# Depthwise convolution of an attention block moved from GpSimd to TensorE, as diagonal matmuls into the bank of the weighted terms

## The chip, the cores and the metric

One core of one Trainium2 chip runs the whole kernel. The metric is the device time of one execution in microseconds (us), taken as the median of several runs. The engines are named as the profile names them: PE is TensorE (PEld its weight loads), DVE is VectorE, ACT is ScalarE, POOL is GpSimd, SP is the engine that issues the DMAs (SPq is its queue). L1195 is line 1195 of the kernel before.

## The reference

The input `x` is (4, 1024, 128): four sequences, which the kernel calls batches, of 1024 tokens and 128 channels in 8 heads of 16. All is float32.

```python
def _ripple(x, Wqkv, Wo, conv_w):
    q, k, v = jnp.split(x @ Wqkv, 3, axis=-1)
    # tele: each token attends to the tokens 0, 1, 2, 4, ... 512 back
    sc = jnp.einsum('bhsd,bhskd->bhsk', qh, kg) / np.sqrt(d)
    w = jax.nn.softmax(jnp.where(valid, sc, -jnp.inf), axis=-1)
    tele = jnp.einsum('bhsk,bhskd->bhsd', w, vg)
    # conv: causal depthwise convolution of v with 7 taps per channel
    vpad = jnp.pad(v, ((0, 0), (KCONV - 1, 0), (0, 0)))
    conv = conv_general_dilated(vpad, conv_w, feature_group_count=c)
    # low: linear attention
    fq, fk = elu(qh) + 1.0, elu(kh) + 1.0
    kv = einsum('bhsd,bhse->bhde', fk, vh)
    low = einsum('bhsd,bhde->bhse', fq, kv) / (z[..., None] + 1e-06)
    return (tele + conv_h + low) @ Wo
x = x + layernorm(xn + _ripple(xn, ...))     # xn = layernorm(x)
x = x + layernorm(moe(layernorm(x)))         # 8 experts of 64, top 2, and a shared one
```

The change is about `conv` alone: `conv[t, c]` is the sum over seven taps of `conv_w[c, tap] * v[t - 6 + tap, c]`.

## The kernel before, in words

Every engine has a program of its own, written out by hand; semaphores join them. The loop runs over five steps `b`. Step `b` holds the attention of batch `b` (steps 0 to 3) and the expert network of batch `b - 1` (steps 1 to 4), cut in two units of 512 tokens, `u0 = 2b - 2` and `u1 = 2b - 1`. The projections of the next batch are made within the step as well. I call the step by its batch.

The attention of a batch has two parts, and the text uses these names for them.

- **The front**, up to the low terms. DVE and POOL multiply q with shifted k (`products`, L263), PE sums them over heads (`sum_heads`, L1163), turns the scores (L1105), DVE makes the softmax (`softmax_logits`, `softmax_weights`, L836 to L856). In the same stretch DVE works through the 24 small steps of the gates of unit u0 (`gates`, L935 to L985, 128x32 elements each), after which PE turns the gates (`gates_expert_major`, L1266), spreads them (`spread_gates`, L1278) and DVE multiplies (`gate_hidden`, L994). `low` (L1181) puts the linear attention into the banks psH and psY, and `weigh_low` (L864) takes it out again and signals `low_used`.
- **The term stage**, from `low_used` on. PE first writes the experts' output of u0 (`experts_out`, L1292, 20 matmuls into psY). Then, tile by tile for eight tiles of 128 tokens, DVE multiplies v with the weights (`weigh`, L880; four sets of buffers, so it can be four tiles ahead) and PE turns and adds the 9 to 12 terms of the tile in psH (`sum_terms`, L1192 and L1195). psH holds four tiles, so it is filled twice, in a first and a second half. After each half `add_conv` (L897, DVE) adds psH and the convolution and writes hT, and `output` (L1206) multiplies it with Wo. Between the tiles PE also runs `project_q`, `project_v` of the next batch, and `hidden`, `gates_expert_major` and `spread_gates` of u1.

`weigh` reads `v_shift`: copies of the token-major v (`v_tok`), shifted by 1 to 64 tokens, which 14 DMAs on SP's queue make (`shift_v`, L339 and L340) as soon as ACT has written `v_tok` at the very end of the batch before. Its first tile waits for all of them.

The convolution runs on POOL, in transposed layout (channels on the partitions): `conv_start` multiplies vT with the last tap, `conv_taps` makes a product (L457, 128x1024) and an addition (L460) for each of the six others, thirteen operations in a chain (`conv_step`). It stands behind `ln3(u1)` in POOL's order. DVE's `add_conv` and ACT's `evacuate_v` of the next batch, which overwrites vT, wait for it.

PSUM is full: psA, psG and psF have two banks each, psH and psY one.

Of the kernel before, what the change touches and what calls it, by code (L numbers as in the profile page):

```python
# [16 lines left out]
ALU = mybir.AluOpType  # L17
# [46 lines left out]
N_CONV_STEPS = 2 * TAPS - 1  # L64
# [49 lines left out]
def block_kernel(nc, x, Wqkv, Wo, conv_w, gate_W, W1, b1, W2, b2, Ws1, bs1, Ws2, bs2, route_scale, out):  # L114
# [4 lines left out]
    with ExitStack() as ctx:  # L119
# [71 lines left out]
        convT = sb("convT", [P, T])  # L191
        tapT = sb("tapT", [P, T])
# [50 lines left out]
        conv_step, hT_ready, y_ready, yc_ready = sem("conv_step"), sem("hT_ready"), sem("y_ready"), sem("yc_ready")  # L243
# [10 lines left out]
        conv_chain = Chain(conv_step, N_CONV_STEPS)  # L254
# [112 lines left out]
        def _(pool):  # L367
# [30 lines left out]
            def more_constants():  # L398
# [18 lines left out]
                nc.gpsimd.memset(neg_half[0:1, 0:1], -0.5).then_inc(consts_ready, 1)  # L417
# [26 lines left out]

            def conv_start(b):
                pool.wait_ge(psA_free, freed(b - 1, PSA_V, 1))
                if b == 0:
                    pool.wait_ge(conv_ld, 16)
                else:
                    pool.wait_ge(hT_ready, upto(b, 2, 0))  # L450
                conv_chain.start(pool, b)
                conv_chain(nc.gpsimd.tensor_scalar(convT[:], vT[:, VPRE:VPRE + T], cw[:, TAPS - 1:TAPS], 0.0,
                                                   ALU.mult, ALU.add))

            def conv_taps(b, shifts):
                for shift in shifts:
                    conv_chain(nc.gpsimd.tensor_scalar(tapT[:], vT[:, VPRE - shift:VPRE - shift + T],  # L457
                                                       cw[:, TAPS - 1 - shift:TAPS - shift], 0.0,
                                                       ALU.mult, ALU.add))
                    conv_chain(nc.gpsimd.tensor_tensor(convT[:], convT[:], tapT[:], ALU.add))  # L460
# [33 lines left out]
            for b in range(B + 1):  # L494
# [12 lines left out]
                if attn:  # L507
                    conv_start(b)
                    conv_taps(b, range(1, TAPS))
                    conv_chain.done()  # L510
# [17 lines left out]
        def _(act):  # L528
# [34 lines left out]
            def evacuate_v(b):  # L563
                act.wait_ge(conv_step, upto(b, N_CONV_STEPS, 0))
                for half in range(2):
                    evacuate(b - 1, PSA_V, half, vT[:, VPRE + half * HALF:VPRE + (half + 1) * HALF])

            def features(b):
# [5 lines left out]
                nc.scalar.activation(fqT[:], qT[:], ACT.Relu).then_inc(q_feat, 1)  # L574

# [104 lines left out]
            for b in range(B + 1):  # L680
# [3 lines left out]
                if attn:  # L684
# [38 lines left out]
                    if ffn:  # L723
                        hidden(u1, range(2, 4))
                        shared_hidden(u1)
# [706 lines left out]
```

## Time and profile before

| | |
|---|---|
| time, median of 3 runs | 341.28 us (341.16 to 342.54) |
| profiled execution: its span, the only time it gives | 339.5 us |
| PE busy | 261.4 us, 77% |
| DVE busy | 275.6 us, 81% |
| ACT busy | 176.8 us, 52% |
| POOL busy | 196.6 us, 58% |
| POOL in L460, the convolution's additions | 57.9 us, 24 of 2412 ns |
| POOL in L457, its products | 30.1 us, 24 of 1255 ns |
| mean granted TensorE clock | 0.874 of full |

A busy share is the part of the span in which the engine had an instruction in work; an instruction that is held by something inside the engine counts as busy, so a small operation with a long duration is a held one. "[2.60 <-DVE gparts L985]" behind a row says that the engine had stood idle for 2.60 us and that DVE's line 985, which writes gparts, ended it. The time outside the profiled span is the difference of the first two lines, 1.8 us; it is taken to stay.

### The profile page before, as it was taken

Reading aid. Unit: us, or ns where it says so; the run is one execution under the profiler, and the core shown is the slowest. Engines: PE = TensorE matmul, PEld = TensorE weight load, DVE = VectorE, ACT = ScalarE, POOL = GpSimd, SP = SyncE. Lnnn points to the kernel's source line nnn. Section 1 sums busy time; section 2 is a strip of 40 time slices with the busy share of each in tenths; the row PEclk is TensorE's granted clock in tenths of the full one; section 3 lists DMA queues with packets and bytes.
Section 4 is the critical chain, followed back from the end, with each engine's and each line's share of the span. In section 5 each row is a group of like instructions: output and inputs, shape, how many; then the busy total and the mean of one; then the engine's idle time right before and its main releaser. Section 6 shows DMA issues by size and latency. Waiting matters only on the chain.

```text
span 339.5 us, 4554 instructions
## 1 busy us (share of the span) xinstructions
PE 261.4 (77%) x1527; PEld 175.7 (52%) x1527; DVE 275.6 (81%) x555; ACT 176.8 (52%) x443; POOL 196.6 (58%) x193
## 2 busy tenths in 40 slices
PE   6666667089379699997788499998795878888894
PEld 6323342087334537667455237767443277685374
DVE  5079866188999999989999999989999999845752
ACT  1683055302538755593569344775484606176852
POOL 4960999601889995306899980327979943131013
PEclk9785996569879959999999659999999559989999
DMA  7200376000025700200049300100248200000003
GB/s 219 71 0 16 106 196 147 24 0 3 9 90 143 215 26 8 69 26 3 37 130 229 111 12 2 31 2 8 84 124 215 83 12 31 0 2 0 2 2 93
DMA packets 20038, 21.89 MB, mean 64 GB/s; under 512 B 3289, under 2 KB 16434, under 8 KB 20014
## 3 DMA queue, kind: packets, MB, share of 16 engines
q1 hardware_dynamic: 20014, 21.59, 22.9%
q8 instruction: 12, 0.20, 0.2%
q14 instruction: 12, 0.10, 0.1%
HBM read 5.07 MB, written 2.10 MB: 21 GB/s over the span
## 4 chain that ended last, share of the span: by engine, by line
DVE 48%; PE 24%; ACT 9%; SPq 7%; DMA 6%; issue 4%; POOL 2%; POOLq 0%; DVEq 0%; ACTq 0%
DVE prods L263 12%; PE psH L1195 7%; DVE prods L880 6%; SPq L340 5%; DMA v_shift<-v_tok 5%; PE psA L1113 3%; DVE hid L994 3%; PE psY L1206 2%; PE psY L1292 2%; PE psA L1105 2%; DVE wgt L853 2%; PE psG L1278 2%; DVE gtmp L966 2%; SPq L339 2%; DVE gtmp L979 2%
## 5 line engine op out<-in xcount | busy, mean ns | idle before, releaser
L421 POOL TENSOR_SCALAR var<-ss 128x4 f32<-128x4 f32 (+1 forms) x25 | 13.4, 538 | 98.9 <-ACT squares L603 46.6
L263 DVE TENSOR_TENSOR prods<-qT,kT 128x1024 f32<-128x1024 f32 x32 | 55.4, 1778 | 12.4 <-ACT qT L530 12.4
L460 POOL TENSOR_TENSOR convT<-convT,tapT 128x1024 f32<-128x1024 f32 x24 | 57.9, 2412 | 2.0
L1195 PE MATMUL psH<-ident,prods 128*128 128x128 f32 x324 | 44.6, 290 | 0.0
L263 POOL TENSOR_TENSOR prods<-qT,kT 128x1024 f32<-128x1024 f32 (+1 forms) x12 | 28.8, 2418 | 23.2 <-PE psA L1163 11.3
L1195 PEld LDWEIGHTS psH<-ident,prods 128*128 128x128 f32 x324 | 40.5, 152 | 2.3 <-issue 2.3
L423 POOL TENSOR_TENSOR rstd<-var,neg_half 128x4 f32<-128x4 f32 (+2 forms) x29 | 37.8, 1305 | 2.4
L1163 PE MATMUL psA<-prods,slot_sel 128*32 128x512 f32 x168 | 26.0, 676 | 12.9 <-DVE prods L263 12.6
L880 DVE TENSOR_TENSOR prods<-v_shift,wgt 128x896 f32<-128x896 f32 x32 | 34.7, 1083 | 0.0
L880 DVE TENSOR_TENSOR prods<-v_tok,wgt 128x128 f32<-128x128 f32 (+2 forms) x60 | 25.8, 456 | 9.9 <-DMA v_shift<-v_tok 9.9
L1113 PE MATMUL psA<-xnT,wqkv 128*128 128x512 f32 x48 | 29.9, 767 | 5.0 <-ACT xnT L530 5.0
L457 POOL TENSOR_SCALAR tapT<-vT,cw 128x1024 f32<-128x1024 f32 x24 | 30.1, 1255 | 2.4
L1256 PE MATMUL psF<-x3T,w 128*128 128x512 f32 x58 | 31.2, 650 | 0.1
L994 DVE TENSOR_TENSOR hid<-hid,psG 128x512 f32<-128x512 f32 x32 | 20.7, 681 | 9.7 <-PE psG L1278 9.1
L1192 PE MATMUL psH<-ident,prods 128*128 128x128 f32 x32 | 9.9, 308 | 15.4 <-DVE prods L880 11.9
L1292 PEld LDWEIGHTS psY<-w,hid 128*128 128x128 f32 x140 | 18.2, 215 | 6.4 <-DVE prods L864 6.4
L1292 PE MATMUL psY<-w,hid 128*128 128x128 f32 x140 | 18.9, 300 | 3.3 <-DVE prods L864 3.3
L603 ACT ACTIVATE squares<-yc 128x128 f32<-128x128 f32 x32 | 9.4, 297 | 22.4 <-DVE yc L903 22.4
L638 ACT ACTIVATE hid<-psF,b1c 128x512 f32<-128x512 f32 x29 | 18.8, 684 | 2.5 <-PE psF L1256 2.4
L1113 PEld LDWEIGHTS psA<-xnT,wqkv 128*128 128x128 f32 x48 | 10.5, 242 | 17.3 <-ACT xnT L530 7.5
L1256 PEld LDWEIGHTS psF<-x3T,w 128*128 128x128 f32 x58 | 10.7, 206 | 13.9 <-issue 13.0
L1163 PEld LDWEIGHTS psA<-prods,slot_sel 128*32 128x32 f32 x168 | 5.3, 118 | 23.5 <-DVE prods L263 13.5
(194 smaller groups left out, 581.3 us busy)
## 6 DMA issues: line engine op xcount, KB each, us to landing
x_in<-L_attn_x SPq DMA_DIRECT2D x4, 512.0 KB, 4.0
x_res<-L_attn_x SPq DMA_DIRECT2D x4, 512.0 KB, 15.3
v_shift<-v_tok SPq DMA_DIRECT2D x4, 508.0 KB
v_shift<-v_tok SPq DMA_DIRECT2D x4, 504.0 KB
v_shift<-v_tok SPq DMA_DIRECT2D x4, 496.0 KB
v_shift<-v_tok SPq DMA_DIRECT2D x4, 480.0 KB
v_shift<-v_tok SPq DMA_DIRECT2D x4, 448.0 KB
out<-y_out SPq DMA_DIRECT2D x7, 256.0 KB, 2.3
```

The source lines that it names most:

```text
L263: return eng.tensor_tensor(prods[:, QUADS * (s % 2) + q, t0:T], qT[:, t0:T], kT[:, PRE - off + t0:PRE - off + T], ALU.mult)
L423: return nc.gpsimd.tensor_tensor(rstd[:, cols], var[:, cols], neg_half[:, cols], ALU.pow)
L457: conv_chain(nc.gpsimd.tensor_scalar(tapT[:], vT[:, VPRE - shift:VPRE - shift + T], cw[:, TAPS - 1 - shift:TAPS - shift], 0.0, ALU.mult, A ...
L460: conv_chain(nc.gpsimd.tensor_tensor(convT[:], convT[:], tapT[:], ALU.add))
L638: nc.scalar.activation(hid[:, c, half_cols(u)], hidden_bank(u, c), ACT.Gelu, bias=b1c[:, c:c + 1]).then_inc(hidden_free, 1)
L880: return nc.vector.tensor_tensor(dst, src.rearrange("p m (h d) -> p m h d", d=HD), w, ALU.mult)
L994: nc.vector.tensor_tensor(hid[:, c, cols], hid[:, c, cols], psG[:, c % 2, :], ALU.mult).then_inc(gated, 1)
L1113: pe.matmul(psA[:, half, :], wqkv[:, bass.ts(part, P)], xnT[:, bass.ts(half, HALF)], start=True, stop=True).then_inc(psA_full, 1)
L1163: ins = pe.matmul(psA[32 * q:32 * q + 32, half, :], ksum_sel[:] if low else slot_sel[:, s, :], fqT[:, cols] if low else prods[:, QUADS * ( ...
L1195: ins = pe.matmul(dst, terms[:, j % TERM_BUFS, m, :], ident[:], is_transpose=True, start=False, stop=(m == live[-1]))
L1256: pe.matmul(hidden_bank(u, c), w1[:, bass.ts(c, P)], x3T[:, half_cols(u)], start=True, stop=True).then_inc(hidden_full, 1)
L1292: ins = pe.matmul(output_tile(u, n), hid[:, c, bass.ts(j, P)], w2[:, c, :], start=(c == CH - 1), stop=(c == CH - 2))
```

## The change

Seven diagonal matrices `tap_diag[:, tap, :]`, the identity times one tap's weights, are made once on POOL. For each half, `sum_conv` has PE multiply them with vT, shifted by the tap, over 512 columns of psH, the first of the seven with `start=True`; the terms of the four tiles are then added on top (`start=False`). `evacuate_h` on ACT copies the sum from psH to hT; `add_conv` is gone from DVE, and the thirteen operations on POOL are gone for each batch. `evacuate_v` waits for `conv_summed` instead.

```diff
@@ POOL, more_constants
-                nc.gpsimd.memset(neg_half[0:1, 0:1], -0.5).then_inc(consts_ready, 1)
+                pool.wait_ge(conv_ld, 16)
+                pool.wait_ge(ident_ready, 1)
+                for tap in range(TAPS):
+                    ins = nc.gpsimd.tensor_scalar(tap_diag[:, tap, :], ident[:], cw[:, tap:tap + 1], 0.0, ALU.mult, ALU.add)
+                ins.then_inc(consts_ready, 1)
...
-                if attn:
-                    conv_start(b)
-                    conv_taps(b, range(1, TAPS))
-                    conv_chain.done()
@@ ACT
+            def evacuate_h(b, half):
+                act.wait_ge(terms_summed, upto(b, NT, TPH * (half + 1)))
+                copy(hT[:, bass.ts(half, HALF)], psH[:]).then_inc(hT_ready, 1)
...
                         shared_hidden(u1)
+                    evacuate_h(b, 0)
+                    if ffn:
                         gates_expert_major(u1)
                         gate_rows(u1)
                     if more:
                         features(b + 1)
                     norm2(2 * b)
+                    evacuate_h(b, 1)
                     if not more:
                         norm3_squares(2 * b)
@@ DVE
-                        if j == TPH:
-                            add_conv(b, 0)
...
                     residual(2 * b)
-                    add_conv(b, 1)
@@ PE
+            def sum_conv(b, half):
+                if half:
+                    pe.wait_ge(hT_ready, upto(b, 2, 1))
+                else:
+                    pe.wait_ge(low_used, b + 1)
+                    if b == 0:
+                        pe.wait_ge(consts_ready, 2)
+                for tap in range(TAPS):
+                    t0 = VPRE - (TAPS - 1 - tap) + half * HALF
+                    ins = pe.matmul(psH[:], tap_diag[:, tap, :], vT[:, t0:t0 + HALF], start=(tap == 0), stop=False)
+                if half:
+                    ins.then_inc(conv_summed, 1)
...
+                        if j % TPH == 0:
+                            sum_conv(b, j // TPH)
                         sum_terms(b, j)
```

On PE, in the term stage of batch 1, the order before is this, from the experts' output to the output of the first half (L1292 are the experts, L1192 and L1195 a tile's terms, L1266 the turned gates, L1206 the output):

```order
L1292 MATMUL psY<-w,hid 128x128 x20
L1192 MATMUL psH<-ident,prods 128x128
L1195 MATMUL psH<-ident,prods 128x128 x8
L1113 MATMUL psA<-xnT,wqkv 128x512 x2
...
L1266 MATMUL psG<-identb,gparts 24x128 x4
L1192 MATMUL psH<-ident,prods 128x128
L1195 MATMUL psH<-ident,prods 128x128 x11
L1206 MATMUL psY<-wo,prods 128x128 x4
```

After the change the same place reads as follows (its lines are those of the changed kernel: L1280 the experts, L1172 the convolution, L1180 and L1183 the terms):

```order
L1280 MATMUL psY<-w,hid 128x128 x20
L1172 MATMUL psH<-vT,tap_diag 128x512 x7
L1180 MATMUL psH<-ident,prods 128x128
L1183 MATMUL psH<-ident,prods 128x128 x8
L1091 MATMUL psA<-xnT,wqkv 128x512 x2
...
L1254 MATMUL psG<-identb,gparts 24x128 x4
L1172 MATMUL psH<-vT,tap_diag 128x512 x7
L1180 MATMUL psH<-ident,prods 128x128
L1183 MATMUL psH<-ident,prods 128x128 x11
L1194 MATMUL psY<-wo,prods 128x128 x4
```

Seven matmuls of 512 columns stand in front of each half's first tile, behind the experts' output in the one place and behind the turned gates in the other.

On ACT, at the end of the term stage, the order before is this (L530 is the copy helper; L603 are the squares of the second norm, L570 to L574 the features of the next batch):

```order
L642 ACTIVATE hid<-gate_shared,bs1c 64x512
L530 ACTIVATE gT<-psG 24x512
L530 ACTIVATE hid<-gT 24x512
L570 ACT_TABLE_LOAD
L570 ACTIVATE kexp<-kT 128x1024
L571 ACTIVATE fkT<-kT 128x1024
L572 ACTIVATE qexp<-qT 128x1024
L574 ACTIVATE fqT<-qT 128x1024
L603 ACTIVATE squares,ss<-yc 128x128 x4
L530 ACTIVATE vT<-psA 128x512 x2
L530 ACTIVATE v_tok<-psA 128x512 x2
```

And after the change:

```order
L626 ACTIVATE hid<-gate_shared,bs1c 64x512
L510 ACTIVATE prods<-psH 128x512
L510 ACTIVATE gT<-psG 24x512
L510 ACTIVATE hid<-gT 24x512
L550 ACT_TABLE_LOAD
L550 ACTIVATE kexp<-kT 128x1024
L551 ACTIVATE fkT<-kT 128x1024
L552 ACTIVATE qexp<-qT 128x1024
L554 ACTIVATE fqT<-qT 128x1024
L587 ACTIVATE squares,ss<-yc 128x128 x4
L510 ACTIVATE prods<-psH 128x512
L510 ACTIVATE vT<-psA 128x512 x2
```

Two copies from psH have come in (hT lies in the space of prods and is named so): one in front of the gates' copy, one in front of the copy of vT.

## Rows read from the trace of the kernel before

**Rows 1.** Page: the span; the engines' shares of the last chain.

```profile
span 339.5 us, 4554 instructions
DVE 48%; PE 24%; ACT 9%; SPq 7%; DMA 6%; issue 4%; POOL 2%; POOLq 0%; DVEq 0%; ACTq 0%
```

**Rows 2.** Windows of batch 1's front and term stage: engines' busy us.

```profile
88.00:130.20 42.20, 31.83 (x157) 15.83 (x154) 40.53 (x70) 26.84 (x66) 38.86 (x27) 0.80 0.34 98
130.20:158.70 28.50, 25.24 (x177) 19.82 (x177) 26.72 (x63) 16.81 (x39) 7.64 (x8) 1.00 0.10 29
```

**Rows 3.** Timeline of DVE and POOL in batch 2's front: start, us, instruction.

```profile
179.08 1.12 POOL L452 TENSOR_SCALAR convT<-vT,cw 128x1024 f32<-128x1024 f32 x1
179.18 1.06 DVE L949 TENSOR_TENSOR gtmp<-gtmp,gmax 128x32 f32<-128x32 f32 x1
...
189.19 2.21 DVE L983 TENSOR_TENSOR gtmp<-gtmp,gparts 128x32 f32<-128x32 f32 x1
```

**Rows 4.** Timeline of PE: the gate turn, batches 1 to 3.

```profile
117.51 0.39 PE L1266 MATMUL psG<-identb,gparts 128*24 128x128 bf16 x4 [2.60 <-DVE gparts L985]
...
191.77 0.58 PE L1266 MATMUL psG<-identb,gparts 128*24 128x128 bf16 x4 [6.19 <-DVE gparts L985]
...
261.07 0.38 PE L1266 MATMUL psG<-identb,gparts 128*24 128x128 bf16 x4 [3.02 <-DVE gparts L985]
```

**Rows 5.** Timeline of PE: the experts' output, batches 1 to 3.

```profile
130.34 4.73 PE L1292 MATMUL psY<-w,hid 128*128 128x128 f32 x40
...
205.73 4.73 PE L1292 MATMUL psY<-w,hid 128*128 128x128 f32 x40 [0.59 <-DVE prods L864]
...
273.80 7.04 PE L1292 MATMUL psY<-w,hid 128*128 128x128 f32 x40 [2.75 <-DVE prods L864]
```

**Rows 6.** Timeline of PE: 512-column matmuls at either clock.

```profile
125.13 3.64 PE L1113 MATMUL psA<-xnT,wqkv 128*128 128x512 f32 x4 [0.78 <-ACT xnT L530]
...
138.71 1.88 PE L1256 MATMUL psF<-x3T,w 128*128 128x512 f32 x4
140.42 0.27 PE L1192 MATMUL psH<-ident,prods 128*128 128x128 f32 x1
```

**Rows 7.** Window in batch 1; last columns: PEclk, DMA share, GB/s.

```profile
126.00:127.00 1.00, 1.00 (x3) 0.34 (x2) 0.93 (x3) 0.00 (x0) 1.00 (x1) 0.50 0.07 28
```

**Rows 8.** Timelines of PE, DVE and SP: the wait for v_shift.

```profile
67.84 0.47 PE L1192 MATMUL psH<-ident,prods 128*128 128x128 f32 x1 [9.85 <-DVE prods L880]
...
66.49 0.29 DVE L880 TENSOR_TENSOR prods<-v_tok,wgt 128x128 f32<-128x128 f32 x1 [9.91 <-DMA v_shift<-v_tok]
...
26.09 0.72 SPq L339 DMA_DIRECT2D v_shift<-v_tok  x1
...
87.97 0.71 SPq L339 DMA_DIRECT2D v_shift<-v_tok  x1
...
158.75 0.70 SPq L339 DMA_DIRECT2D v_shift<-v_tok  x1
```

**Rows 9.** Timelines of PE and DVE: the second half's sums.

```profile
142.40 0.33 PE L1192 MATMUL psH<-ident,prods 128*128 128x128 f32 x1 [0.61 <-DVE prods L880]
...
145.07 0.30 PE L1192 MATMUL psH<-ident,prods 128*128 128x128 f32 x1 [0.93 <-DVE prods L897]
...
219.25 0.30 PE L1192 MATMUL psH<-ident,prods 128*128 128x128 f32 x1 [0.55 <-DVE prods L897]
...
155.21 0.68 DVE L897 TENSOR_TENSOR prods<-psH,convT 128x512 f32<-128x512 f32 x1
```

**Rows 10.** Timeline of ACT: a copy of half a bank; batch 3's end.

```profile
136.96 0.60 ACT L530 ACTIVATE qT<-psA 128x512 f32<-128x512 f32 x1 [0.70 <-PE psA L1113]
...
299.64 1.28 ACT L734 ACT_TABLE_LOAD   x1
...
302.07 0.31 ACT L603 ACTIVATE squares<-yc 128x128 f32<-128x128 f32 x1 [0.94 <-DVE yc L903]
```

**Rows 11.** Timeline of POOL: batch 0's first products.

```profile
19.08 4.57 POOL L263 TENSOR_TENSOR prods<-qT,kT 128x512 f32<-128x512 f32 x2 [1.38 <-ACT qT L530]
```

More of the change, by code:

```diff
@@ L63 @@
 N_SOFTMAX_STEPS = 5
-N_CONV_STEPS = 2 * TAPS - 1
 N_FRONT = 3
@@ L190, in block_kernel @@
         prods = sb("prods", [P, 2 * QUADS, T])
-        convT = sb("convT", [P, T])
-        tapT = sb("tapT", [P, T])
+        tap_diag = sb("tap_diag", [P, TAPS, P])
         space = prods[:].rearrange("p a t -> p (a t)")
@@ L242, in block_kernel @@
         terms_ready, terms_summed = sem("terms_ready"), sem("terms_summed")
-        conv_step, hT_ready, y_ready, yc_ready = sem("conv_step"), sem("hT_ready"), sem("y_ready"), sem("yc_ready")
+        conv_summed, hT_ready, y_ready, yc_ready = sem("conv_summed"), sem("hT_ready"), sem("y_ready"), sem("yc_ready")
         ss2_ready, x2_ready, ss3_ready, xn3_ready = sem("ss2_ready"), sem("x2_ready"), sem("ss3_ready"), sem("xn3_ready")
@@ L253, in block_kernel @@
         softmax_chain = Chain(softmax_step, N_SOFTMAX_STEPS)
-        conv_chain = Chain(conv_step, N_CONV_STEPS)
         def bank(tile):
@@ L443, in products @@
                             product(nc.gpsimd, s, q).then_inc(pool_prod_ready, 1)
[L445 to L460, printed above, removed]
             def ln2(u):
@@ L563, in evacuate_v @@
             def evacuate_v(b):
-                act.wait_ge(conv_step, upto(b, N_CONV_STEPS, 0))
+                act.wait_ge(conv_summed, upto(b, 1, 0))
                 for half in range(2):
@@ L891, in weigh @@
                 beside(2)
-            def add_conv(b, half):
-                dve.wait_ge(terms_summed, upto(b, NT, TPH * (half + 1)))
-                dve.wait_ge(conv_step, upto(b, N_CONV_STEPS, N_CONV_STEPS))
-                cols = bass.ts(half, HALF)
-                nc.vector.tensor_tensor(hT[:, cols], psH[:], convT[:, cols], ALU.add).then_inc(hT_ready, 1)
             def add_normed(b, half):
@@ L1182, in low @@
                 ins.then_inc(low_ready, 1)
+            def sum_conv(b, half):
[10 more added lines that the diff above has]
+                    ins.then_inc(conv_summed, 1)
             def sum_terms(b, j):
                 pe.wait_ge(terms_ready, upto(b, NT, j + 1))
-                if j == 0:
-                    pe.wait_ge(low_used, b + 1)
-                elif j == TPH:
-                    pe.wait_ge(hT_ready, upto(b, 2, 1))
                 dst = psH[:, bass.ts(j % TPH, P)]
-                pe.matmul(dst, low_terms[:, j, :], ident[:], is_transpose=True, start=True, stop=False)
+                pe.matmul(dst, low_terms[:, j, :], ident[:], is_transpose=True, start=False, stop=False)
                 live = [m for m in range(NV) if TERMS[m] < P or TERMS[m] // P <= j]
@@ L1195, in sum_terms @@
                     ins = pe.matmul(dst, terms[:, j % TERM_BUFS, m, :], ident[:], is_transpose=True,
-                                    start=False, stop=(m == live[-1]))
+                                    start=False, stop=(m == live[-1] and j % TPH == TPH - 1))
                 ins.then_inc(terms_summed, 1)
```

## The prediction

> **What bounds the kernel now.** I read the page first: the span is 339.5 us, and in the chain that ended last DVE has 48% and PE 24% [rows 1], POOL hardly any. So POOL's 88 us of convolution are not on the chain by themselves. The windows then tell two kinds of stretch apart [rows 2]: in the front of batch 1 DVE is busy 40.5 of 42.2 us and PE 31.8 at a mean granted clock of 0.80; in the term stage that follows DVE is busy 26.7 and PE 25.2 of 28.5 at full clock. The reader is to see that PE has no room in the second stretch, which is where the change puts its matmuls, and that DVE seems to have none in the first.
>
> But part of DVE's time in the front is not work. In batch 2 a gate step of 128x32 elements takes 1.06 us and another 2.21; the first ends at 180.24, just when POOL's convolution operation, begun before it, ends (180.20) [rows 3]. A DVE operation with two SBUF inputs is held until POOL's ends. Seven of batch 2's steps are held, of which the rows show the first and the last. What this costs stands on PE: the turn of the gates came after 2.60, 6.19 and 3.02 us of idle time that the last gate step ended [rows 4]. Low terms are through when the experts' output starts: 130.34, 205.73 and 273.80 [rows 5].
>
> **The price of the new matmuls.** Four records of PE are two matmuls of 128x512, with different weights: they start at 138.71 and the next work at 140.42, so one matmul takes 0.86 us at full clock [rows 6]. Seven make 6.0 us a half, 12.0 a batch, 48 in all. At the low clock, granted clock 0.50, which is the 1.2 GHz level [rows 7], the same two took 3.64 [rows 6], so a half would cost up to 12.
>
> One page reads otherwise. The Trainium skill (TensorE: Matmul & The Clock Gate, Back-to-back issue gap) gives about 131 ns as the sustained spacing of matmuls of 512 columns; the row has 0.43 us for each record. By the page a half would cost 14 x 0.131 = 1.8 us and the sum would turn negative; by the row it is 6.0. The row is of this very shape and type, so the sum goes by it.
>
> **Batch 0.** The first half's convolution waits for low_used and the constants. PE is then idle for 9.85 us before 67.84, since the shifted copies land only at 66.49 [rows 8]; 6.0 us fit, cost nothing. Without that cover they would cost 6.0. The second half stands behind the first four tiles with only the wait for the copy before it, which stays: +6.0. PE's idle stretch is shorter, so the first tiles may run at the higher clock earlier; I take 0.5 off, bounds 0 and 2: **+5.5**.
>
> **Batch 1, front.** With POOL quiet, the last gate step is early and the 2.60 us in front of the gate turn go [rows 4]. They are all that goes: the turn cannot come before PE's work in front of it. From the turn (117.51) to low_used (130.2) it took 12.7. I rebuild this chain at full clock: turn and copy of the gates 1.2, two spreads 1.0, gate_logits 0.9, two spreads 1.0, last product 0.8, softmax sums and weights 4.0, low terms 1.3, together 10.2. These are estimates from the same operations at full clock; PE, with no idle time of 2.6 us there, should keep it, where before the clock was 0.50 [rows 7]. That gives 2.5 more, bounds 0 and 3. Low_used is 5.1 earlier. PE then does the experts' output and the first half's convolution, +6.0, so the first tile's sum starts 0.9 later than before. DVE has its terms ready by then: the copies took 40.4 us from the first issue to the use (26.09 to 66.49), so those issued from 87.97 land at 128.4 [rows 8], and with 2.4 for the first tile that is 5 us before the convolution's end at 136.0 (135.1 and 0.9).
>
> **Batch 1, term stage.** The second half costs 6.0 less what PE idled: 0.61 before the fourth tile and part of the 0.93 at the second half's first sum, where DVE's copy was late ([rows 9], against 0.55 in batch 2). I take 5.0, bounds 4.5 and 6. At the end add_conv stood behind the residual without idle time [rows 9]; ACT is free there, I take 0.5 off (bounds 0 and 1). Batch 1: 0.9 + 5.0 - 0.5 = **+5.4**.
>
> **Batch 2.** The turn gains 6.19 [rows 4], the chain behind it, 13.8 long, 3.5: low_used is 9.7 earlier, at 196. The copies, issued from 158.75 [rows 8], land at 199.2, before experts (4.7) and convolution (6.0) are through at 206.7. So -9.7 + 6.0 = -3.7; then +6.0 for the second half, whose wait of 0.55 [rows 9] stays, and -0.5: **+1.8**.
>
> **Batch 3.** The turn gains 3.02 [rows 4] and the chain 2.5: -5.5, and +6.0. The experts' output took 7.04 against 4.73 [rows 5], because PE had been idle 2.75 before; whether the clock holds this time is open, I take half of the 2.3: -1.2. Second half +6.0, less 1.3 for idle time and low clock at the last tiles (bounds 0 and 3): together **+4.0**.
>
> **The end.** ACT's copy of the last half takes 0.60 [rows 10] like DVE's addition, so the swap itself is nothing in the chain. But in batch 3 the squares and the table load (299.64, 1.28) now stand behind this copy instead of before the sum's end. Copy, four squares and table make about 3.9 us, where the squares of the last unit had started 2.8 after the last sum (302.07, with 0.94 idle, [rows 10]): **+1.1**, bounds 0 and 1.5.
>
> **Costed at nothing.** The seven diagonals on POOL: between nothing and 1.12 each (the 128x1024 form, [rows 3]), so at most 7.8 us after which POOL's first products, now at 19.08 [rows 11], come at most 6.5 late; batch 0's wait of 9.85 hides this, else it is that. ACT's copy of the first half waits in front of the gates' copy and, in batch 0, of the next batch's features; these are needed only at the batch's end. DVE loses eight operations of 0.68 [rows 9], off the path but for what is counted. Nobody waits for the time that POOL gets back.
>
> **Sum.** 5.5 + 5.4 + 1.8 + 4.0 + 1.1 = 17.8. The span becomes 357.3; with the 1.8 between the profiled span and the median, 359.1, that is 5% slower. In short: 48 us of PE work, of which 6 hide in batch 0, about 20 are paid by the front and about 4 by idle time and late copies.
>
> **The rivals.**
> - *The front gives nothing back*, because something else (ACT's work, or PE at the low clock) holds the chain to low_used at its old length. For it: PE's clock was 0.80 in the front [rows 2], and ACT has its own queue there. Against: three idle times are named after the gate step [rows 4]. Then the front's 5.1, 9.7 and 5.5 are lost too: 359.1 + 20.3 = 379. With the idle times alone gained, 11.8 of the 20.3, it is 367.6, which is still inside my case.
> - *The copies become the bound.* If they land later than 40.4 after issue by more than 5 us, each of three batches is later by the rest. One engine's share, 0.07, is all that moves at the end of a landing [rows 7]. The Trainium skill (DMA: Bandwidth & Descriptors, Why a DMA increments its semaphore by 16 and not by 1) says that a transfer over 127 partitions uses one engine; the trace agrees with the share of 0.07. I see nothing in the change that slows it; 3 us in each would give 368.
> - *The other side: a convolution matmul is cheaper than a projection's.* If 512 columns went at 0.13 us a record, a half costs 1.8 and the copies' landing bounds the fronts: first sums start 4.3, 8.9 and 4.3 earlier (landing plus 2.4 for the first tile, 130.8 and 201.6, against 135.1 and 210.5, [rows 5, 8]; batch 3 like batch 1), and the second halves cost 1.8 x 4 less about 1. With the end's 1.1, that is -17.5 + 6.2 + 1.1 = -10.2: 331. It decides from about 0.25 us a record on. For it speaks only the page cited above; against it every 512-column row.
> - *The held steps go on being held* by POOL's remaining work. Then it is the first rival.
>
> **How the numbers follow.** A difference under 0.5%, 1.7 us, is about what a measurement of this kernel can't tell from none. My case 0.84, front gives nothing 0.06, copies bound 0.05, the cheap matmul 0.04, anything else about even 0.01. Within my case the bounds add up as follows: all at their kind end (3.5 less in batch 0 and 3's clock, 3 in the last tiles and idle times, 1.1 at the end, 1.5 elsewhere) gives 350; the chain behind the turn not quickened (8.5 more), the low clock in batch 3 and no idle time regained (2.5) gives 370. The range 350 to 369 leaves out the far rivals and the edge. Slower 0.94, within 0.5% 0.02, faster 0.04.
>
> **What would show it.** PE busy up by about 45 us, to over 300; twice seven 512-column matmuls a batch at 0.86 us spacing; no gate step over 0.3 us while POOL is idle; low_used 5 to 10 us earlier relative to the batch's first copy issue; then no idle time on PE from the experts' output to the second half's end; the term stages longer by about 11 us in batches 1 to 3, by 6 in batch 0. Wrong would be the prediction if the fronts stay 42 to 47 us long (the chain isn't the gates'), if the new matmuls take 1.7 us (the clock falls), or if DVE and not PE ends the waits in the term stage.

## The result and the profile after

The changed kernel takes **359.87 us** (median of 4 runs, 358.91 to 360.02) where the kernel before took 341.62 in runs on the same chip: ratio 1.0542, interval 1.0502 to 1.0583. It is 5.4% slower. Its profiled span is 358.2 us, against 339.5 [rows 1].

The page of the changed kernel: the span, the engines' busy us with their shares and instructions, the chain that ended last, and the new matmuls as a group (busy us, mean ns, idle time before).

```profile
span 358.2 us, 4710 instructions
PE 298.7 (83%) x1639; PEld 190.2 (53%) x1639; DVE 237.2 (66%) x547; ACT 181.0 (51%) x451; POOL 112.3 (31%) x147
...
PE 53%; ACT 18%; DVE 11%; SPq 7%; DMA 6%; POOL 3%; issue 2%; POOLq 0%; DVEq 0%; ACTq 0%
...
L1172 PE MATMUL psH<-vT,tap_diag 128*128 128x512 f32 x112 | 49.8, 595 | 1.8 <-ACT prods L510 1.8
```

The chain has turned over: before, DVE had 48% and PE 24% [rows 1]; now PE has 53%. The new matmuls take 49.8 us and almost never wait; they are on the path, not in gaps.

The windows of the changed kernel: batch 1's stage from the experts to the next batch's first copy, and the last microseconds of the fronts of batches 1 and 2. After the busy times come PEclk, DMA share, GB/s.

```profile
131.10:169.50 38.40, 36.95 (x206) 25.02 (x204) 23.10 (x60) 17.82 (x41) 7.04 (x7) 1.00 0.08 23
126.00:130.00 4.00, 4.00 (x6) 1.70 (x7) 3.69 (x6) 1.44 (x3) 0.00 (x0) 0.57 0.06 26
202.00:208.00 6.00, 5.24 (x6) 2.19 (x7) 4.37 (x6) 3.18 (x6) 0.00 (x0) 0.50 0.34 109
```

The stage that took 28.5 us with both engines nearly full [rows 2] takes 38.4 us with PE at 96% and DVE at 60%. The two lower rows matter below: there the granted clock is at or near 0.50, the 1.2 GHz level.

The timeline of SyncE, the first copy of each batch, answers to the issues in [rows 8]; that of batch 3 stood at 233.08 before.

```profile
26.61 0.73 SPq L336 DMA_DIRECT2D v_shift<-v_tok  x1
...
92.96 0.70 SPq L336 DMA_DIRECT2D v_shift<-v_tok  x1
...
169.51 0.71 SPq L336 DMA_DIRECT2D v_shift<-v_tok  x1
...
247.30 0.71 SPq L336 DMA_DIRECT2D v_shift<-v_tok  x1
```

From issue to issue the batches grew by 4.5 (batch 0), 5.8 and 3.5 us; batch 3, to its last sum, by 4.0; the head and the end by 0.5 each. That is the 18.7 us of the span, with rounding.

The timeline of PE in the changed kernel, batch 1 (start, us, instruction, idle before and what ended it).

```profile
119.59 0.39 PE L1254 MATMUL psG<-identb,gparts 128*24 128x128 bf16 x4
...
122.16 1.10 PE L1223 MATMUL psF<-x3T,w 128*128 128x512 f32 x2 [0.62 <-ACT x3T L510]
...
124.71 0.41 PE L1228 MATMUL psF<-ident,gate_shared 8*128 8x8 f32 x4 [0.92 <-ACT gate_shared L510]
...
125.89 3.55 PE L1091 MATMUL psA<-xnT,wqkv 128*128 128x512 f32 x4 [0.77 <-ACT xnT L510]
129.24 2.05 PE L1244 MATMUL psF<-x3T,w 128*128 128x512 f32 x4
131.13 4.63 PE L1280 MATMUL psY<-w,hid 128*128 128x128 f32 x40
135.59 6.17 PE L1172 MATMUL psH<-vT,tap_diag 128*128 128x512 f32 x14
141.60 0.27 PE L1180 MATMUL psH<-ident,prods 128*128 128x128 f32 x1
...
150.37 6.28 PE L1172 MATMUL psH<-vT,tap_diag 128*128 128x512 f32 x14 [0.36 <-ACT prods L510]
```

Fourteen records are seven matmuls: 135.59 to 141.60 is 6.0 us a half, at full clock. The turn of the gates (L1254), which stood behind 2.60 us of idle time [rows 4], has none. In VectorE's timeline the low terms end here:

```profile
129.15 0.68 DVE L851 TENSOR_TENSOR prods<-psY,wgt 128x512 f32<-128x512 f32 x1
```

That is 129.83, 36.9 us behind the batch's first copy issue, where it was 42.3. But the experts start only at 131.13: PE was still at its own queue, projection and first hidden chunks at the low clock.

### The profile page after: what moved, and what is told of

Read it like the earlier page. It is cut to its first block, busy times and chain, and to the rows that moved or that the text cites. A ratio compares the mean times of both kernels' runs of the same rounds, so it can differ in the third digit from the quotient of the medians.

```text
span 358.2 us, 4710 instructions
## 1 busy us (share of the span) xinstructions
PE 298.7 (83%) x1639; PEld 190.2 (53%) x1639; DVE 237.2 (66%) x547; ACT 181.0 (51%) x451; POOL 112.3 (31%) x147
## 4 chain that ended last, share of the span: by engine, by line
PE 53%; ACT 18%; DVE 11%; SPq 7%; DMA 6%; POOL 3%; issue 2%; POOLq 0%; DVEq 0%; ACTq 0%
PE psH L1172 12%; PE psH L1183 10%; PE psA L1091 6%; DVE prods L260 5%; PE psY L1280 5%; SPq L337 5%; PE psF L1244 5%; DMA v_shift<-v_tok 5%; ACT xn L522 3%; PE psA L1141 2%; ACT xn L600 2%; PE psY L1194 2%; ACT prods L510 2%; SPq L336 2%; ACT hid L622 2%
## 5 line engine op out<-in xcount | busy, mean ns | idle before, releaser
L260 DVE TENSOR_TENSOR prods<-qT,kT 128x1024 f32<-128x1024 f32 x32 | 53.3, 1714 | 13.0 <-ACT qT L510 13.0
L1172 PE MATMUL psH<-vT,tap_diag 128*128 128x512 f32 x112 | 49.8, 595 | 1.8 <-ACT prods L510 1.8
L1183 PE MATMUL psH<-ident,prods 128*128 128x128 f32 x324 | 41.5, 278 | 0.0
L1183 PEld LDWEIGHTS psH<-ident,prods 128*128 128x128 f32 x324 | 37.7, 144 | 4.3 <-issue 4.3
L867 DVE TENSOR_TENSOR prods<-v_tok,wgt 128x128 f32<-128x128 f32 (+2 forms) x60 | 20.8, 373 | 26.6 <-DMA v_shift<-v_tok 23.0
L260 POOL TENSOR_TENSOR prods<-qT,kT 128x1024 f32<-128x1024 f32 (+1 forms) x12 | 30.9, 2591 | 19.6 <-PE psY L1194 11.7
L1172 PEld LDWEIGHTS psH<-vT,tap_diag 128*128 128x128 f32 x112 | 20.6, 189 | 26.1 <-issue 23.3
L1091 PE MATMUL psA<-xnT,wqkv 128*128 128x512 f32 x48 | 29.6, 762 | 3.3 <-ACT xnT L510 3.3
L510 ACT ACTIVATE prods<-psH 128x512 f32<-128x512 f32 x8 | 4.8, 597 | 35.4 <-PE psH L1183 35.4
L1280 PEld LDWEIGHTS psY<-w,hid 128*128 128x128 f32 x140 | 18.2, 212 | 3.4 <-DVE prods L851 2.4
L1280 PE MATMUL psY<-w,hid 128*128 128x128 f32 x140 | 18.5, 297 | 0.9 <-DVE prods L851 0.9
L1091 PEld LDWEIGHTS psA<-xnT,wqkv 128*128 128x128 f32 x48 | 10.1, 233 | 15.6 <-issue 6.3
## 6 DMA issues: line engine op xcount, KB each, us to landing
x_res<-L_attn_x SPq DMA_DIRECT2D x4, 512.0 KB, 15.5
```

The source lines that it names most:

```text
L260: return eng.tensor_tensor(prods[:, QUADS * (s % 2) + q, t0:T], qT[:, t0:T], kT[:, PRE - off + t0:PRE - off + T], ALU.mult)
L867: return nc.vector.tensor_tensor(dst, src.rearrange("p m (h d) -> p m h d", d=HD), w, ALU.mult)
L1091: pe.matmul(psA[:, half, :], wqkv[:, bass.ts(part, P)], xnT[:, bass.ts(half, HALF)], start=True, stop=True).then_inc(psA_full, 1)
L1172: ins = pe.matmul(psH[:], tap_diag[:, tap, :], vT[:, t0:t0 + HALF], start=(tap == 0), stop=False)
L1183: ins = pe.matmul(dst, terms[:, j % TERM_BUFS, m, :], ident[:], is_transpose=True, start=False, stop=(m == live[-1] and j % TPH == TPH - 1))
L1280: ins = pe.matmul(output_tile(u, n), hid[:, c, bass.ts(j, P)], w2[:, c, :], start=(c == CH - 1), stop=(c == CH - 2))
```

## The experiments

Each run's ratio is to the kernel before, run on the same chip; I turn differences of ratios into time with 340.3 us. "Relative" times are counted from the batch's first copy issue.

### 1. The old load back on GpSimd, the new matmuls kept

```diff
+        tapT = sb("tapT", [P, T])
...
+                if attn:
+                    conv_start(b)
+                    conv_taps(b, range(1, TAPS))
+                    conv_chain.done()
```

`conv_start` is one product and `conv_taps` six products and six additions, all within the one scratch buffer tapT, which nobody reads. The copy of the next batch's v waits for them again.

> The changed kernel, with POOL doing its old thirteen operations per batch again in their old place, into a scratch buffer that nobody reads (one buffer instead of two, for want of space; the result is that of the changed kernel). My theory: the fronts were shortened by 4.2, 7.6 and 5.8 us because POOL no longer holds DVE. All three come back, so the time is 359.9 + 17.6 = 377, between 372 and 380, with gate steps of 1 to 2.2 us and idle time on PE in front of the gate turn as before. Rival (the fronts are shorter because PE's clock or order changed, POOL has no part): 360, unchanged, with the gate steps held but the front as short.

Measured 371.0 us (370.05 to 372.38), ratio 1.0909 (1.086 to 1.0958): 12.5 us more than the change, some 5 short of the expectation. The timeline of PE in this kernel, the turn of the gates in batches 1 to 3:

```profile
122.77 0.39 PE L1275 MATMUL psG<-identb,gparts 128*24 128x128 bf16 x4 [1.68 <-DVE gparts L987]
...
205.65 0.58 PE L1275 MATMUL psG<-identb,gparts 128*24 128x128 bf16 x4 [4.83 <-DVE gparts L987]
...
283.85 0.38 PE L1275 MATMUL psG<-identb,gparts 128*24 128x128 bf16 x4 [2.09 <-DVE gparts L987]
```

The idle times of [rows 4] are back, a little smaller: 1.68, 4.83, 2.09 for 2.60, 6.19, 3.02. So is the hold of single steps; VectorE in batch 2:

```profile
197.22 1.55 DVE L964 TENSOR_TENSOR gtmp<-gtmp,gmax 128x32 f32<-128x32 f32 x1
198.81 0.19 DVE L966 TENSOR_TENSOR gtmp<-gtmp 128x32 f32<-128x32 f32 x1
```

A step of 128x32 takes 0.19 or, held, 0.78 to 1.77. That GpSimd's load lengthens the fronts, through held steps, is shown: with it the experts start 3.3, 5.0 and 3.5 us later behind the first copy issue than in the change, which had them 4.2, 7.6 and 5.8 us earlier than the kernel before. Why not all came back is argued and not shown: the 24 additions within one buffer took 1.98 us each, where the two-buffer ones had taken 2.41, so this load holds VectorE for less time than the real convolution did.

### 2. No convolution at all

```diff
-                for tap in range(TAPS):
-                    t0 = VPRE - (TAPS - 1 - tap) + half * HALF
-                    ins = pe.matmul(psH[:], tap_diag[:, tap, :], vT[:, t0:t0 + HALF], start=(tap == 0), stop=False)
                 if half:
+                    ins = pe.transpose(psH[:, 0:P], ident[:], ident[:])
...
```

The convolution's part of the output is missing here. Each tile's low terms start the bank themselves again, and one turn of the identity a batch stands for the signal.

> The changed kernel without the convolution: the 14 matmuls per batch are left out, the terms of each tile start the bank themselves; the output lacks conv. My theory: seven of the eight halves are on the path at 6.0 us each, 42 in all, of which the landing of the shifted copies, the first tiles' terms and DVE's pace take back 1 to 4: 320, between 316 and 325, which is 18 to 25 below the kernel before. Rival (PE is not the bound of the term stages, DVE is): the time falls by less than 25, to over 335.

Measured 325.86 us (323.96 to 328.2), ratio 0.9582 (0.9522 to 0.9642), just above the 325 that the expectation allowed. The new matmuls thus cost 32.7 us net of their 49.8. In the traces the batches are 5.8, 9.5, 12.2 and 6.2 us shorter than in the change, where the matmuls take 12.0 in each. VectorE's first term in batch 1 of this kernel:

```profile
127.41 0.29 DVE L867 TENSOR_TENSOR prods<-v_tok,wgt 128x128 f32<-128x128 f32 x1 [0.73 <-DMA v_shift<-v_tok]
```

and PE's first sums in batches 0 and 1:

```profile
68.69 0.45 PE L1178 MATMUL psH<-ident,prods 128*128 128x128 f32 x1 [12.29 <-DVE prods L867]
...
132.45 0.27 PE L1178 MATMUL psH<-ident,prods 128*128 128x128 f32 x1
```

In batch 0 the landing of the copies holds the first sum, as it does in the change, so the first half's 6 us save nothing. In batch 1 VectorE waits for the copies but PE doesn't: its first sum follows the experts without idle time, so the landing is not the bound there. What is missing in batch 1 goes with the front: two matmuls at its start took 2.07 us, at the low clock, for 1.13 in the change, and the low terms came 2.5 us later behind the first issue. I didn't trace it further. In batch 2 PE waits 0.68 us for VectorE's terms. In batch 3 it waits 3.5 us in all for terms that start at the landing, besides a wait of 1.44 that stands in the change too.

### 3. Four taps of seven

```diff
-                for tap in range(TAPS):
+                for tap in range(3, TAPS):
...
```

The first of the four starts the bank. Three taps' part of the convolution is left out.

> The changed kernel with the last four of the seven taps; three are left out. My theory: linear in the matmuls on the path, 3 taps x 0.86 us x 7 halves = 18.1 less: 342, between 340 and 345. Rival (the copies' landing or DVE's pace already bounds at four taps): 348 or more. A clock rival: fewer matmuls let the granted clock fall and the gain is eaten, 346 or more.

Measured 343.65 us (341.38 to 345.52), ratio 1.0086 (1.0046 to 1.0127). Three taps less save 15.5 us, 5.2 a tap; 0.86 us in each of the seven halves that nothing hides would be 6.0. At that rate break-even with the kernel before would lie near 3.4 fp32 taps, which is an estimate; fewer than four were not run.

### 4. The same matmuls in bfloat16

```diff
-        tap_diag = sb("tap_diag", [P, TAPS, P])
+        tap_diag = sb("tap_diag", [P, TAPS, P], BF16)
...
-                    ins = pe.matmul(psH[:], tap_diag[:, tap, :], vT[:, t0:t0 + HALF], start=(tap == 0), stop=False)
+                    high = vT[:, t0:t0 + HALF].bitcast(BF16).rearrange("p (t h) -> p t h", h=2)[:, :, 1]
+                    ins = pe.matmul(psH[:], tap_diag[:, tap, :], high, start=(tap == 0), stop=False)
```

The weights and (by taking the upper half of each word) the values of the convolution are of bfloat16 precision.

> The changed kernel with the convolution in bfloat16: the diagonals are bfloat16, and vT is read through a view of the high half of each float32 (v cut to bfloat16, so conv is less exact). My theory: one record of 0.215 us per tap instead of two of 0.43, so 1.5 us a half instead of 6.0: 7 x 4.5 = 31.6 less, of which DVE's pace and the landing take back up to 4: 330, between 327 and 335, faster than the kernel before by 2 to 4%. Rival (reading every second 16-bit element or the bfloat16 matmul costs as much as float32): 345 or more. If PE's lighter load lets the clock fall in the first half: up to 338.

Measured 331.38 us (329.09 to 332.42), ratio 0.9751 (0.9703 to 0.98): 8.5 us faster than before and 26.9 faster than the change by the ratios. Its PE timeline, first half of batch 1:

```profile
131.61 1.53 PE L1173 MATMUL psH<-vT,tap_diag 128*128 128x512 bf16 x6
132.98 0.27 PE L1181 MATMUL psH<-ident,prods 128*128 128x128 f32 x1
```

The record of one of the seven is missing, the first by all signs: the six that are there fill 131.61 to 132.98 evenly, 1.37 us, so a matmul takes 0.23 us, for 0.86 in fp32, and a half 1.6. The instructions, the semaphores between them and what GpSimd is rid of are those of the change; the matmul's type alone turns its sign. It is also the prediction's rival "a convolution matmul is cheaper", which had worked out 331: it had the first sums 4.3, 8.9 and 4.3 us earlier than before, held by the landing, and they came 2.1, 8.3 and 4.3 earlier. But PE goes from the experts through the convolution to the first sum without idle time in batches 1 to 3, so the experts' start set them and not the landing. That the number came out so close is in part luck.

### 5. TensorE kept busy in the fronts

```diff
                         spread_gates(u0, range(2, 4))
+                        keep_busy(8, front(u1, LOGITS))
                         turn_logits(u1)
+                        keep_busy(8, hidden_bank(u1, 0))
```

> The kernel of the change with two lines more in each front of batches 1 to 3: eight 128x128 turns of the identity on TensorE ahead of the second unit's turned logits and eight behind them, into banks that are free there, to fill the gaps of 0.6, 0.9 and 0.8 us in front of L1223, L1228 and L1091. Nothing of the result changes. Theory (in batches 1 and 2 the front's last 1.3 and 2.4 us are TensorE's own queue, because the granted clock fell to half after those gaps): the granted clock of the stretch from the second unit's logits to the first expert product rises above the 0.50 to 0.61 of the changed kernel, project_k's four records take about 1.9 us instead of 3.55 to 3.78, the experts start within 0.3 us of the end of the weighted low terms (they started 1.30 and 2.43 us behind it), and the experts of batch 3, 6.8 us for 40 records, come down towards 4.7. Together 1.3 + 2.4 + about 2, less some 0.3 us for each batch that the fill itself takes: span 353.5 from 358.2, time about 355 (353 to 358). Rival (the clock of this stretch doesn't follow the gaps, or the fill delays the logits by as much as it saves): no change, 358.5 to 361.

Measured 356.03 us (355.42 to 358.57), ratio 1.0459 (1.0414 to 1.0504), 2.8 us below the change by the ratios; the two intervals just touch, so the size is uncertain. The edit fills two of the three gaps, those in front of L1228 and L1091. The traces show the mechanism. PE in batch 1 of this kernel:

```profile
126.57 1.09 PE L1289 MATMUL psF<-ident 128*128 128x128 f32 x8
127.50 1.91 PE L1091 MATMUL psA<-xnT,wqkv 128*128 128x512 f32 x4
129.24 1.88 PE L1244 MATMUL psF<-x3T,w 128*128 128x512 f32 x4
131.39 0.82 PE L1280 MATMUL psY<-w,hid 128*128 128x128 f32 x5 [0.27 <-DVE prods L851]
```

and in batch 3, where the changed kernel's experts had taken 6.80:

```profile
280.45 4.73 PE L1280 MATMUL psY<-w,hid 128*128 128x128 f32 x40 [2.00 <-DVE prods L851]
```

The gap of 0.63 us in front of L1223 is still there, and the granted clock stays at 1.00 all the same, from 123 us to the experts. The projection takes 1.91 for 3.55 us, and the experts start 0.05 us behind the low terms in batches 1 and 2, where it was 1.30 and 2.43. Batch 2 is 2.2 us shorter for it and batch 3 1.9. In batch 1 only 0.4 comes through (its front's earlier part ran 0.7 later here), and batch 0, which the edit doesn't touch, lost 1.3: there three tiles' sums ran at the low clock (1.91, 2.13 and 2.08 us for 1.91, 1.59 and 1.25).

### 6. Bfloat16 and fill together

> The bfloat16 diagonals and values of the fourth kernel (331.4 us) and the fill of the run before, together. The weights and the values of the convolution are rounded to bfloat16, all else is computed as before. If the fill's gain stands by itself, it is the same few us here, less what the copies of v_shift (landing 39.5 to 40.9 us behind their first issue, against a first term at 40.8, 39.4 and 39.8) now hold back: the fronts can't get ahead of them, so at most about 1 us for each of batches 1 and 2 comes through. Theory: 329 us (327 to 331). Rival (the fill brings nothing, or the copies hold all of it): 330.5 to 333. Slower than 333 would mean that the fill itself stands on the path.

Measured 330.46 us (328.67 to 331.76), ratio 0.9688 (0.9648 to 0.9729), not to be told from the fourth kernel. VectorE's first term waits for the copies in every batch (11.8, 2.5, 1.9 and 5.4 us), as it does in the change (11.9, 3.2, 2.6 and 5.3), so that wait by itself tells nothing. PE is what shows the bound: its first sum waits 11.3 us in batch 0, not at all in batches 1 and 2, and 1.35 us in batch 3.

### 7 and 8. The copy by one partition, cut in two

The first copy of each batch, the one shifted by one token, covers 127 partitions (508 KB). In the changed kernel one window of batch 0, long after its issue:

```profile
58.00:62.00 4.00, 4.00 (x10) 1.51 (x8) 0.00 (x0) 0.00 (x0) 0.00 (x0) 1.00 0.06 26
```

A DMA share of 0.06 is one engine of 16, at 26 GB/s. The view doesn't name the copy; cutting it in two tells. SyncE's issues behind that copy show more:

```profile
27.38 8.00 SPq L337 DMA_DIRECT2D v_shift<-v_tok  x1
...
50.76 0.99 SPq L337 DMA_DIRECT2D v_shift<-v_tok  x1
```

The next issue takes 8.0 us and another 5.4, where most take one or two, and the last copy is issued 24 us behind the first.

```diff
-N_SHIFT_DMA = 16 * 2 * len(SHIFTS)
+N_SHIFT_DMA = 16 * (2 * len(SHIFTS) + 1)
...
-                    sp.dma_start(v_shift[off:P, n], v_tok[0:P - off]).then_inc(v_shifted, 16)
+                    cut = 112 if off == 1 else P - off
+                    sp.dma_start(v_shift[off:off + cut, n], v_tok[0:cut]).then_inc(v_shifted, 16)
+                    if off == 1:
+                        sp.dma_start(v_shift[off + cut:P, n], v_tok[cut:P - off]).then_inc(v_shifted, 16)
```

> The kernel of the change with the copy that moves 127 partitions by one (508 KB) cut in two, of 112 and of 15 partitions; nothing of the result changes. In the changed kernel one of the 16 DMA engines alone is busy from 58 to 68 us (share 0.06, 26 GB/s) while all others are done: that copy's tail, 508 KB at 26 GB/s being 19.5 us. Theory (batch 0's first half of the convolution lies hidden behind this landing, as the prediction had it, and in batches 1 to 3 the landing at 39.6 to 40.2 us decides nothing): the last copy lands at about 32 us behind the first issue instead of 40.1, batch 0's first sum starts where its first half of the convolution ends, at about 62.1 us instead of 68.5, with the first three tiles' sums perhaps 1 us faster by a clock that doesn't fall. Batches 1 to 3 as before. 6.4 to 7.7 us less: about 353 from 359.9 (351 to 355). Rival (the cut copy lands no earlier, because the engine is held by all copies together): 359 to 361. If batches 1 to 3 gain too, over 2 us each, the landing did hold them and the prediction's reading of them was wrong: below 350.

Measured 351.4 us (350.08 to 352.92), ratio 1.032 (1.0274 to 1.0366), 7.6 us less than the change by the ratios. PE in batch 0 of this kernel:

```profile
54.57 6.17 PE L1175 MATMUL psH<-vT,tap_diag 128*128 128x512 f32 x14
60.58 0.27 PE L1183 MATMUL psH<-ident,prods 128*128 128x128 f32 x1
60.69 1.04 PE L1186 MATMUL psH<-ident,prods 128*128 128x128 f32 x8
```

The sum follows the convolution at once and at full clock. Batch 0 is 8.6 us shorter; batches 1 to 3 are as in the change (77.0, 78.0 and 70.5 us for 76.6, 77.8 and 70.3), although VectorE no longer waits for a copy in any of them. So the landing held batch 0, and nothing else. The Trainium skill (DMA: Bandwidth & Descriptors, Why a DMA increments its semaphore by 16 and not by 1) gives the reason: a transfer over 127 partitions is put on one engine. The trace agrees, with the share of 0.06, and the cut removes that tail.

> The bfloat16 diagonals and values, the fill, and the cut copy together. The weights and the values of the convolution are rounded to bfloat16. With a convolution of 1.5 us a half, batch 0's first sum waits for the copies alone (11.3 us of idle TensorE): with a landing at about 32 us it starts some 8 us earlier, 60.5 instead of 68.9, and its first tiles' sums run at the high clock (1 us). In batches 1 and 2 the first sum waits for the experts, so nothing; in batch 3 the first term stood at 40.3 and the experts' end at 39.7, so at most 0.5. 330.5 less 8.5 to 9.5: about 321.5 (319 to 324). Rival (the cut copy lands no earlier): 329.5 to 331.5.

Measured **312.67 us** (312.5 to 313.51), ratio 0.9188 (0.9147 to 0.9229), 9 us below the expectation and the fastest of all. PE in batch 0:

```profile
55.07 1.53 PE L1176 MATMUL psH<-vT,tap_diag 128*128 128x512 bf16 x6
56.44 0.27 PE L1184 MATMUL psH<-ident,prods 128*128 128x128 f32 x1
```

Its last issue of a copy, and two windows of batch 0 (PEclk, DMA share, GB/s at the end):

```profile
42.31 0.60 SPq L340 DMA_DIRECT2D v_shift<-v_tok  x1
```

```profile
46.00:50.00 4.00, 1.61 (x11) 1.15 (x10) 3.06 (x3) 2.50 (x5) 0.00 (x0) 0.99 0.51 155
50.00:54.00 4.00, 4.00 (x7) 1.48 (x6) 3.86 (x6) 1.24 (x3) 0.00 (x0) 0.59 0.00 0
```

The last copy is issued 16.2 us behind the first, and nothing moves from 50 to 54 us: all have landed within 24 us relative, before VectorE's low terms are done, where I had put 32. So the first sum stands at 30.4 relative and not at about 34: 11.7 us gained there, and 1.8 in tiles at the high clock. Batch 1 gave 1.6 us back. Batch 3 is 5.6 us shorter, of which I had counted 0.5: before, its first two sums waited 1.35 and 2.06 us for VectorE's late terms, and the hidden chunks behind them then took 3.37 us at the low clock; here the sums don't wait and the chunks take 1.88.

### 9. The kernel before, with the cut copy

> The kernel before the change with the same cut of the copy by one partition, in 112 and 15 partitions; nothing of the result changes. It shows what the change costs when no copy hides any of it. Before, batch 0's first sum waits for the copies from 57.9 to 67.8 us, while GpSimd's convolution runs until 65.4. With the cut copy the first sums start near 58 and are done by about 63, and adding the convolution then waits for GpSimd until 65.4, so that the first half's sum is there at about 66.1 instead of 76: 9.5 us less; in batches 1 to 3 the first sum waits for the experts, which start at 42 to 47 us, behind the landing at 40, so nothing. Theory: 340.2 - 9.5 = 330.7 (329 to 333), and the change with the cut copy (351.4) then costs 20.7 us where it cost 18.2 to 18.3 with the uncut one. Rival (the front of batch 0 gains all of 11 us or more and its end is not held by GpSimd): 328 or below. Second rival (GpSimd's convolution, running beside the terms, holds VectorE's terms back): 334 to 337.

Measured 339.52 us (339.06 to 341.82, 12 runs), ratio 0.9984 (0.9953 to 1.0014): **nothing gained**, which none of the three forecasts had. VectorE in batch 0 of this kernel:

```profile
60.29 2.79 DVE L883 TENSOR_TENSOR prods<-v_tok,wgt 128x256 f32<-128x256 f32 x2
62.99 1.92 DVE L883 TENSOR_TENSOR prods<-v_shift,wgt 128x896 f32<-128x896 f32 x1
...
69.38 2.91 DVE L883 TENSOR_TENSOR prods<-v_tok,wgt 128x384 f32<-128x384 f32 x2
...
73.81 0.74 DVE L883 TENSOR_TENSOR prods<-v_tok,wgt 128x384 f32<-128x384 f32 x2
```

and GpSimd beside it:

```profile
46.12 2.37 POOL L463 TENSOR_TENSOR convT<-convT,tapT 128x1024 f32<-128x1024 f32 x1
...
59.30 3.29 POOL L463 TENSOR_TENSOR convT<-convT,tapT 128x1024 f32<-128x1024 f32 x1
...
68.60 3.07 POOL L463 TENSOR_TENSOR convT<-convT,tapT 128x1024 f32<-128x1024 f32 x1
```

and TensorE behind the half's end:

```profile
74.28 2.55 PE L1198 MATMUL psH<-ident,prods 128*128 128x128 f32 x11
...
76.62 1.92 PE L1209 MATMUL psY<-wo,prods 128*128 128x128 f32 x8
...
78.33 2.78 PE L1116 MATMUL psA<-xnT,wqkv 128*128 128x512 f32 x4
```

In the kernel before, the convolution's last addition and the sum of the half were these:

```profile
63.04 2.34 POOL L460 TENSOR_TENSOR convT<-convT,tapT 128x1024 f32<-128x1024 f32 x1
...
75.50 0.69 DVE L897 TENSOR_TENSOR prods<-psH,convT 128x512 f32<-128x512 f32 x1 [1.56 <-PE psH L1195]
```

The terms start at 56.6, ten microseconds earlier, but while the convolution runs a pair that takes 0.74 alone takes 2.91, and the addition takes 3.07 to 3.29 for 2.37. The convolution ends at 71.7 (before: 65.4), and the half's sum is added at 73.2 (before: 75.5, with the first copy issued 0.9 earlier). Of the 9.5 us that I had expected 3.2 are left by then. They are lost to the clock: TensorE, idle between the terms, does the next tile's sum, the output and the projection at the low clock, in 2.55, 1.92 and 2.78 us for 1.36, 1.06 and 1.88, which is 3.0 more. Batch 0's last sum ends 58.05 us behind the first issue, for 58.30 before. The second rival had the first of the two mechanisms, and put the loss at 3 to 6 us. It was about 9, some 6 by contention and 3 by the clock.

So the change, which cost 5.4% with the uncut copy, costs 3.4% (1.032 over 0.9984, 11.4 us) with the cut one. I had expected 20.7 us.

### 10. The fastest kernel without its fill

> The kernel of bfloat16 diagonals and values with the cut copy, without the fill of the fronts: the weights and the values of the convolution are rounded to bfloat16. It shows what the fill is worth here, where TensorE's clock after the gaps may or may not fall. With the fill it took 312.7 us. In the kernel of bfloat16 without fill the experts of batch 1 started 1.3 us behind the weighted low terms and those of batches 2 and 3 at once. Theory (the clock falls after the gaps in some batches): 314 to 316. Rival (as between the two uncut kernels of bfloat16, no measurable difference): 311.5 to 313.5.

Measured 315.68 us (313.02 to 315.83), ratio 0.9252 (0.921 to 0.9294) against 0.9188 (0.9147 to 0.9229): the difference, 2.2 us, is within what the intervals allow, so it is not shown by the times. The traces have the experts 1.30 us behind the low terms in batches 1 and 2 without fill and 0.05 with it, and those intervals 1.1 us shorter each.

## Why the prediction was right, step by step

- **The price of the matmuls** held: 6.0 us a half. The fourth run shows that this term carries the sign. The 131 ns that the prediction took from the Trainium skill (TensorE: Matmul & The Clock Gate, Back-to-back issue gap) for a matmul of 512 columns is not borne out here: in fp32 a record took 0.43 us, in bfloat16 a matmul took 0.23.
- **Batch 0: +5.5 predicted, 4.5 measured**, and 0.5 in front of it that had been costed at nothing. The first half lay in the copies' wait: PE still idled 6.34 us behind it. The seventh run took that cover away: there the sum follows the convolution at once. The first tiles gained 1.4 by the clock where 0.5 had been taken.
- **The fronts: right to low_used, off behind it.** It was earlier by 5.45, 9.93 and 5.81 us (predicted 5.1, 9.7, 5.5). The first run gives 3.3, 5.0 and 3.5 us of the experts' earlier start back. But the step "PE, with no idle time of 2.6 us there, should keep" the clock failed: gaps of 0.62, 0.92 and 0.77 us stood in front of L1223, L1228 and L1091, the granted clock behind them was 0.50 to 0.57, and the experts came 1.3 and 2.4 us behind the low terms. Filling the last two gaps removed it.
- **Batch 1: +5.4, measured 5.8. Batch 2: +1.8, measured 3.5**, of which 2.4 is this mis-sized step; something under 1 us elsewhere gave a part back, and I didn't trace it. **Batch 3: +4.0, measured 4.0**, its experts still at the low clock: 6.80 us for a predicted half-way 5.9.
- **The end: +1.1, measured 0.5.** The squares start 3.6 us behind the last sum for 2.7 before; ACT's order is as foreseen, and 0.4 came back behind it.
- **Costed at nothing**: the diagonals on POOL take 0.65 us each, and its first products come at 22.15 instead of 19.08 [rows 11], without effect.
- **The signs.** PE's busy time was to rise by about 45 us, to over 300; it rose by 37, to 298.7, since its other work took 12.5 us less, at a mean granted clock of 0.924 for 0.874. The term stage of batch 1 grew by 9.9 us for about 11. No gate step is held in the fronts, and between the experts' output and the second half PE idles 0.36 us in batch 1, for ACT's copy.
- **The rivals.** "The front gives nothing back" is refuted by the first run's reverse. "The copies become the bound" holds in no batch of the change but batch 0, where it was counted; where the matmuls were gone or cheap (second, fourth and sixth run), late terms held PE in batch 3 too, for 1.8 to 3.5 us. "The cheap matmul" is true of bfloat16 and false of fp32.

The total of 359.1 against 359.87 owes something to errors that cancel: batch 0 and the end too dear by 1.1 with the head counted in, batches 1 and 2 too cheap by 2.1.

## What to carry to other kernels

Moving work from an idle-looking engine to a matmul is decided by the price of one instruction in that type and shape, read from a row of the same kernel: at 0.86 us it lost 18 us, at 0.23 it won 8 or 9. Work on GpSimd that runs beside VectorE costs on both engines, though the chain of waits names neither; a wait that seems to hold the path may only cover that contention, and taking it away then gains nothing until the contention is gone too (cut copy: nothing before the change, 7.6 us after it, 17 with bfloat16 as well). Before taking a long transfer for the bound, look whether one DMA engine alone carries its end: here one copy of 127 partitions did, and held up the issue of the others.

## What the runs showed of the hardware that I had not expected

- A copy over 127 partitions of 508 KB set the landing at 40 us behind the first issue. Its tail on one engine and the 8.0 us that the issue behind it took both went with the cut, and which of them weighed more was not separated. Cut in two, all copies landed within 24 us.
- VectorE's operations of two SBUF inputs and GpSimd's addition slow each other: 0.74 to 2.91 us for a pair on the one side, 2.37 to 3.29 on the other, without a wait in the profile. Longer operations suffer less in proportion (1.08 to 1.92 for 896 elements).
- Three gaps of 0.6 to 0.9 us on TensorE were followed by a granted clock of 0.50 that lasted through four or more records of full work (projection 3.55 for 1.91 us). With sixteen turns of the identity in the last two gaps it stayed at 1.00, the first gap of 0.63 us still there.
